# Four order constants of a cross-network kernel: where VectorE takes a chunk's product and a group's column preparation

## The reference, cut to what matters

```python
def _L0_rec_ref(inputs, f0, f1, f2):          # inputs: (512, 39, 16)
    x0 = inputs
    xk = inputs
    outs = []
    for W in [f0, f1, f2]:                    # (39*39,128), (128*39,128), (128*39,128)
        b, f, d = x0.shape
        g = xk.shape[1]
        z = jnp.einsum('bfd,bgd->bfgd', x0, xk).reshape(b, f * g, d)
        cur = jnp.einsum('bpd,pm->bmd', z, W)
        outs.append(cur)
        xk = cur
    return jnp.sum(jnp.concatenate(outs, axis=1), axis=-1)
...
h = jnp.concatenate([z, dense_ctx], axis=1)
h = jnp.maximum(h @ W_top1 + b_top1, 0.0)
h = jnp.maximum(h @ W_top2 + b_top2, 0.0)
y = h @ W_top3
```

## Time and profile before

| | |
|---|---|
| runs (median; lowest to highest) | 804.95 us; 803.73 to 805.82 |
| the profiled execution | 804.9 us; its span, from first to last instruction, 803.1 us |
| busy share of the span | TensorE 91%, VectorE 79%, GpSimd 67%, ScalarE 44% |
| TensorE's granted clock, mean | 0.987 of full |
| before tile 0's layer 2 | 0 to 65.0 us |
| tiles 0 to 15 | 65.0 to 774.1 us |
| behind the last bank | 774.1 to 803.1 us |

### The profile page before, as it was taken

How to read it: one execution, slowest core, us unless ns; L and a number is a source line. 1 busy time by engine, 2 the same in 40 slices (tenths; PEclk the granted TensorE clock), 3 DMA queues, 4 the chain that set the end, 5 groups by cost and what they waited for, 6 DMA issues and landing times.

```text
span 803.1 us, 11565 instructions
## 1 busy us (share of the span) xinstructions
PE 730.2 (91%) x3392; PEld 582.3 (73%) x3392; DVE 630.7 (79%) x1962; ACT 357.0 (44%) x1048; POOL 535.9 (67%) x512
## 2 busy tenths in 40 slices
PE   3998889888999999988999999988999998989977
PEld 3966667667777877767787887767777886868757
DVE  7857888877988479986988569886898569898960
ACT  3224444444554345544554254544554344545531
POOL 6746989876797558876797558864475536666540
PEclk9999999999999999999999999999999999999989
DMA  9350000000000000000000000000000000000000
GB/s 220 56 199 3 5 4 4 3 3 3 2 3 3 2 3 2 3 3 2 3 3 2 2 3 2 3 1 1 0 1 2 1 0 1 1 1 2 1 1 1
DMA packets 12959, 11.15 MB, mean 14 GB/s; under 512 B 3937, under 2 KB 11841, under 8 KB 12643
## 3 DMA queue, kind: packets, MB, share of 16 engines
q1 hardware_dynamic: 8352, 9.24, 4.4%
q0 software_dynamic: 4544, 1.17, 1.8%
HBM read 10.40 MB, written 0.00 MB: 13 GB/s over the span
## 4 chain that ended last, share of the span: by engine, by line
PE 57%; DVE 22%; issue 8%; POOL 8%; ACT 2%; DMA 1%; SPq 0%; DVEq 0%; POOLq 0%; ACTq 0%
DVE scaled L640 16%; PE y L796 10%; PE y L798 10%; PE y L797 9%; PE side L814 4%; PE side L803 3%; POOL emb L341 3%; PE y L862 3%; PE acc L778 3%; PE acc L772 3%; PE acc L773 3%; PE rep L763 2%; DVE diag L649 2%; POOL z_parts L351 2%; DVE z L609 2%
## 5 line engine op out<-in xcount | busy, mean ns | idle before, releaser
L640 DVE SCALAR_TENSOR_TENSOR scaled<-y,x_rows,scaled 128x128 f32<-128x128 f32 x1728 | 468.5, 344 | 123.0 <-PE y L798 91.7
L467 ACT ACTIVATE scaled<-y,x_rows 128x128 f32<-128x128 f32 x768 | 218.3, 367 | 170.0 <-PE y L798 168.3
L796 PE MATMUL y<-w_hi,x_parts 128*128 128x512 f32 (+1 forms) x640 | 272.5, 426 | 1.6 <-DVE x_parts L615 1.3
L798 PE MATMUL y<-w_hi,x_parts 128*128 128x512 f32 (+1 forms) x640 | 249.6, 390 | 0.0
L797 PE MATMUL y<-w_lo,x_parts 128*128 128x512 f32 (+1 forms) x640 | 249.5, 390 | 0.0
L351 POOL TENSOR_TENSOR z_parts<-z,z_parts 128x512 fp32r<-128x512 f32 x109 | 147.9, 1357 | 132.2 <-ACT z_parts L413 131.6
L341 POOL DMA_INDIRECT emb<-in_tbl_dram,ids_sb x142 | 140.9, 992 | 31.0 <-issue 19.2
L796 PEld LDWEIGHTS y<-w_hi,x_parts 128*128 128x128 f32 x640 | 121.4, 190 | 34.1 <-issue 4.3
L798 PEld LDWEIGHTS y<-w_hi,x_parts 128*128 128x128 f32 x640 | 121.0, 189 | 25.6
L413 ACT ACTIVATE z_parts<-z 128x512 fp32r<-128x512 f32 x112 | 70.8, 634 | 153.9 <-DVE z L609 153.9
L797 PEld LDWEIGHTS y<-w_lo,x_parts 128*128 128x128 f32 x640 | 121.6, 190 | 24.3 <-issue 0.2
(11 more groups left out here) (88 smaller groups left out, 554.8 us busy)
## 6 DMA issues: line engine op xcount, KB each, us to landing
w_sb<-in_w_dram SPq DMA_DIRECT2D x1, 2496.0 KB, 9.1
emb<-in_tbl_dram,ids_sb POOLq DMA_INDIRECT x142, 2.4
s_sb<-in_w_dram SPq DMA_DIRECT2D x12, 160.0 KB
w_sb<-in_small_tables_dram SPq DMA_DIRECT2D x1, 980.0 KB
wt_sb<-in_W_top_dram SPq DMA_DIRECT2D x1, 768.0 KB, 10.4
s_sb<-in_w_dram SPq DMA_DIRECT2D x4, 144.0 KB
diag<-in_selectors_dram SPq DMA_DIRECT2D x1, 532.0 KB, 8.2
wt_sb<-in_W_top_dram SPq DMA_DIRECT2D x1, 512.0 KB, 11.0
```

The costliest lines, as they stand in the source:

```text
L467: done = act.activation(scaled[:, k % 2, BY_ACT.index(j), i * M:(i + 1) * M], y2[n % RING][:, i * M:(i + 1) * M], ACT.Copy, scale=x0_rows[ ...
L640: dve.scalar_tensor_tensor(part, y2[n % RING][:, i * M:(i + 1) * M], x0_f, part, ALU.mult, ALU.add).then_inc(terms_in, 1)
L796: pe.matmul(dst, x1_hi[:, t % 2, cols], hi, start=True, stop=False)
L798: pe.matmul(dst, x1_lo[:, t % 2, cols], hi, start=False, stop=True).then_inc(y_ready, 1)
```

## The change

Three edits, all of order. No instruction is added, removed or resized, and no wait names another condition than before, but for the position in the lists.

```diff
-PROD_LAG = 1
+PROD_LAG = 0
...
-T_AT = (10, 13, 20, 23)
+T_AT = (10, 14, 20, 24)
...
-                    if q == 2 and g + 1 < GROUPS and s - 2 in T_AT:
-                        columns_lo(g + 1, T_AT.index(s - 2))
+                    if q == 2 and g + 1 < GROUPS and s - 1 in T_AT:
+                        columns_lo(g + 1, T_AT.index(s - 1))
```

## The result

The changed kernel took 769.24 us in the median of 4 runs (766.02 to 771.06), the kernel before 805.38 (4 runs). The ratio is 0.954, with an interval of 0.951 to 0.956. 769.3 had been forecast, within 763 to 788. The profiled execution took 770.4 us, with a span of 768.6. The page of the kernel after, part 1, beside the earlier trace rows: every engine's busy time stays within 6 us, and the span is 34.5 shorter.

What follows compares the result with a forecast made beforehand. No engine full; a loop over VectorE and TensorE through product(1) sets each tile. Savings 12.5 + 3.3 + 12.9 + 3.0 + 2.2 + 1.7 = 35.6 from 804.9 give 769.3 us, range 763 to 788.

Steps and rivals of the forecast that it cites:

- GpSimd's stream starts 1.64 earlier: Tiles 0 and 1 go by GpSimd's stream of gathers, so together they gain only its earlier start, 1.64 us.
- r3_out: Tiles 4, 8, 12: product(4) ahead of bank 17 ends TensorE's wait for r3_out; 3.0 us, bounds 0 to 3.0.
- replicate(4): Tiles 11, 13, 14: product(3) ahead of spread_rows ends replicate(4)'s wait; 2.2 us, bounds 0 and 2.2.
- Rival 1: Column preparation: its stalls move instead of going, without 12.9 and 1.7 the time is 784.0 us; chance 0.13.
- The loop through product(1): VectorE's run before product(1), which replicate(2) follows: one bank less saves 1.04 us in each of tiles 3 to 14, 12.5.
- columns_lo ahead of spread_rows: Tiles 2, 6, 10: columns_lo behind banks 11 and 21, steps four banks apart, ends six columns_t stalls; 12.9 us.
- The 0.5 a tile: Deduction in each of three preparation tiles: spread_rows delays columns_lo of step 1, for which slot 18's s_block waits.
- The clock: Tile 10: with the stall of 2.3 gone, the 3.4 us at the lower clock behind it goes; 1.7 us.
- GpSimd, with some 3 us a tile unused in its stream, stays short of full too: Products' part, shown on tile 5: GpSimd has room, so each of tiles 3 to 14 gains the 1.04 us.
- The rule that the prediction set against the change: Exclusive SBUF lock: earlier product(0) brings low_part(0) next to slot 2's spread_rows, giving back 0.2 to 2.2 us a tile.
- the fourth: VectorE stands at products 0, 4 and 5, waiting for their replicate: slower, 828.7 us; chance 0.09.
- a sign of being wrong: VectorE idle ahead of L609, 0.1 in the kernel before, would show VectorE standing at products.

Runs made afterwards that it cites:

- changed_again: The changed kernel with no edit, run again on a third chip: 770.17 us, ratio 0.955.
- experiment 4: The changed kernel with product(1) put back to slot 5: 808.51 us, ratio 0.981.
- (3): The kernel before with only product(1) moved, to slot 4: 817.43 us, ratio 0.996.
- (7): The changed kernel with DIAG_AT = (12, 30), so spread_rows leaves slot 2: 780.34 us, ratio 0.946.
- experiment 10: The kernel before with only product(4) moved, to slot 16; a single run, tiles sum to 707.6 us.
- all_but_product_1: The run of experiment 4: the changed kernel with product(1) put back to slot 5, 808.51 us, ratio 0.981.
- only_product_1: The kernel before with one product of seven moved, product(1), to slot 4: 817.43 us, ratio 0.996.
- Experiment 5: The changed kernel with spread_rows of slot 12 put back ahead of product(3) in tiles 3 to 9: 788.72 us, ratio 0.959.
- experiments 2: The kernel before with only the column preparation changed (T_AT, columns_lo one slot behind columns_hi), products as before: 807.93 us, ratio 0.981.
- 11: The changed kernel with T_AT = (10, 13, 20, 23) as before; a single run, tiles 2, 6, 10 at 43.9, 44.5, 44.5 us.
- experiment 6: The changed kernel with GpSimd's gathers spread otherwise over slots and tiles: 785.54 us, ratio 0.955.
- spread_and_gathers: The changed kernel with spread_rows at slots 12 and 30 and the gathers spread otherwise: 772.23 us, ratio 0.934.
- best_again: The changed kernel with spread_rows at slots 12 and 30 and gathers spread otherwise, run again on a third chip: 757.82 us, ratio 0.940.

## Why the prediction was right

By tiles, forecast and measured, in us taken off:

| tiles | terms | forecast | measured |
|---|---|---|---|
| 0 and 1 | GpSimd's stream starts 1.64 earlier | 1.6 | 1.7 (1.4 in changed_again) |
| 2 | loop 1.64, columns 4.7 | 6.3 | 6.4 |
| 6 | loop 1.04, columns 4.7 | 5.7 | 6.1 |
| 10 | loop 1.04, columns 3.5, clock 1.7 | 6.3 | 6.5 |
| 4, 8, 12 | loop 1.04, r3_out 1.0 each | 6.1 | 6.5 |
| 3, 5, 7, 9 | loop 1.04 each | 4.2 | **2.3** |
| 11, 13, 14 | loop 1.04, replicate(4) 0.73 each | 5.3 | 5.7 |
| sum | | 35.6 | 35.1 |

The head was 1.5 shorter and the tail 2.0 longer than in the profile of before, which nearly cancels; no edit touches either. The mechanism and the sizes of most terms were right; that 769.24 lies within 0.1 of the forecast is luck, as a term 1.9 too large was made up for by others that came out too small. (Rival 1's time is 783.9 by its own terms, not 784.0.)

- *The loop through product(1)* is shown from both sides: one product moved back costs 0.99 to 1.06 in every tile from 2 on that the clock leaves alone (experiment 4), that product alone moved gives 1.02 to 1.05 in tiles 4, 8 and 12 (3), and taking spread_rows out of the same run gives 0.8 in tiles 11 to 14 (7).
- *columns_lo ahead of spread_rows*: right in place and size. The 0.5 a tile that I took off for a late columns_lo of step 1 was not paid: no s_block of slot 18 waits in tiles 2, 6 and 10. In tile 6 spread_rows took 0.82 in place of the 2.12 with which I had walked it. It came just ahead of GpSimd's L366, and there it was L366 that took longer, 1.31 in place of 0.74:

```profile
339.29 1.31 POOL L366 TENSOR_TENSOR sum<-sum 128x256 f32<-128x256 f32 x1
```

- *r3_out* and *replicate(4)*: right in size. The first is shown by experiment 10. For the second, all_but_product_1 has product(3) ahead of spread_rows and product(1) where it was: replicate(4) doesn't wait, and tiles 11 and 13 are 0.9 shorter than before (forecast 0.73). But in only_product_1 the wait went as well, with product(3) behind spread_rows, which fell to 0.82. So product(3)'s place is not the only thing that ends it, and product(3) alone was not moved.
- *The clock* (1.7 in tile 10): the stall that the dip followed is gone, and so is the dip. Where such a stretch fell in other runs it cost 1.3 to 1.6. But that term belongs to the profile that I started from and not to the kernel: in the kernels that keep these stalls (1.5 to 3.1 us by the rows) a dip fell in tiles 2 and 10, or 2 and 6, or in all three. What the change takes away is the chance of it.
- *What failed* is a clause: "GpSimd, with some 3 us a tile unused in its stream, stays short of full too". It had no slack where it counted. In tile 5 of the kernel before it waits 1.65, 1.19 and 0.33 us for others, 3.2 in all, but each of these waits lies ahead of low_part(2) or ends with it. From there its stream runs, in tiles 3, 5, 7 and 9, with gaps of under 0.2 us to the x2 that the s_block of slot 38 waits for, and the moved spread_rows lengthened it by 0.48. The loop's term is too large by 1.9 for these four tiles. The rest of the tiles came in 0.05 to 0.4 above their terms and made up for most of it.

The rule that the prediction set against the change (the Trainium skill, SBUF — State Buffer, section Who interferes with whom: two SBUF inputs on VectorE against a GpSimd instruction that reads SBUF, an exclusive lock) did cost something, but at the other spread_rows, the one of slot 12 which I had taken as covered; in slot 2 it took 0.88 to 0.91 in tiles 3 to 14 (1.22 in tile 2), as before. Experiment 5 agrees with the rule that the two shut each other out: 2.15 and 1.22 where the two tensor_tensors meet, 0.81 and 0.75 where they don't. On the order it is less clear: by its start in the trace spread_rows came 0.16 ahead of L364 and yet was the one that waited.

Of the rivals, the fourth left a trace: VectorE, which never waited for a replicate ahead of L609 in the tiles, now does four times (tiles 0, 4, 8 and 12), for 2.8 us in all. The prediction had named this as a sign of being wrong; tiles 4, 8 and 12 nonetheless came out 2.15 to 2.18 shorter, of 2.04 forecast. Of the first rival experiments 2 and 11 leave nothing.

Still open: in experiment 6, by pairs of tiles, the gathers' leaving gave 0.63 to 0.70 in three of four cases, and spread_rows' meeting accounts for 0.47 of it; the other 0.2 was not separated. Nor was it tested why tiles 0 and 1 gained so little from fewer gathers, and why tile 2 lost 1.0 there.

## What to carry to other kernels

Where two engines hand each other one bank, find in the trace the instruction that always starts a constant few hundredths behind another engine's, and list what stands ahead of that other one in its gapless run: each such piece is paid once a tile, wherever the engine idles otherwise. Price a reordering by tile and not by engine totals, and for each piece that moves look at what runs beside it at its new time: here the same spread_rows took 0.82 or 2.15, by what GpSimd did. A third engine's busy share says nothing of its slack: count it from the event that starts its gapless stretch to the one that waits for its end.

## What the hardware showed

- A stall of TensorE of 2.0 us was at times followed by 3.4 us at the lower clock (1.2 GHz, matmuls 0.43 apart in place of 0.23): in all_but_product_1 behind the stall in tiles 6, 8, 10, 12 and 14, and not behind the equal one in tiles 4, 5, 9 and 13. So lengthening this stall by 1.04 cost 2.4 to 2.6 in the five tiles, and single profiles can differ by some 1.5 us for each such stretch.
- Where VectorE's spread_rows met a GpSimd instruction, either could be the one that took longer: spread_rows 2.15 us in place of 0.82 (changed kernel, tile 5, started 0.16 ahead of L364), a tensor_tensor on GpSimd 1.31 in place of 0.74 (tile 6, started 0.10 behind spread_rows), a gather 1.44 to 1.46 in place of 0.96 (only_product_1, tiles 3, 5, 7 and 9, started 0.2 behind). A gather that had started 0.15 ahead of it cost neither anything (kernel before, tile 5).
- The head of one and the same kernel took 77.7 us on one chip and 63.9 on another (spread_and_gathers and best_again), while its tiles summed to 660.9 and 660.2. Each chip was used at one time only, so the two can't be told apart.
